# A decoder layer on one core: the feed-forward's quantised input turned by a transfer, its products moved behind other work

## The reference

```python
def activation_quant(x):                      # a row to 8 bits
    s = 127 / clip(max(abs(x), axis=-1, keepdims=True), 1e-5)
    return clip(round(x * s), -128, 127) / s

def ffn(x, w_gate, w_up, w_down, ln_weight):  # weights: ternary, scaled by mean(abs(w))
    h = silu(activation_quant(x) @ qw_gate.T) * (activation_quant(x) @ qw_up.T)   # 256 -> 1024
    h = rms_norm(h, ln_weight)
    return activation_quant(h) @ qw_down.T    # 1024 -> 256

x = x + mixer(layernorm(x), ...)              # projections x, z, B, C, dt; conv; ssd; gate; rms; W_out
x = x + cross_attention(layernorm(x), ctx_2048, ...)
x = x + ffn(layernorm(x), ...)
```

## Time and profile before

| | us |
|---|---|
| median of 3 runs | 1201.06 (1199.09 to 1201.66) |
| the profiled execution, time | 1197.11 |
| its span, first to last instruction | 1195.0 |
| PE busy | 1130.4 (95%) |
| DVE busy | 1003.0 (84%) |
| POOL busy | 930.7 (78%) |
| ACT busy | 824.2 (69%) |

### The profile page before, as it was taken

How to read it: one execution, slowest core, us unless ns; L and a number is a source line. 1 busy time by engine, 2 the same in 40 slices (tenths; PEclk the granted TensorE clock), 3 DMA queues, 4 the chain that set the end, 5 groups by cost and what they waited for, 6 DMA issues and landing times.

```text
span 1195.0 us, 34853 instructions
## 1 busy us (share of the span) xinstructions
PE 1130.4 (95%) x11463; PEld 976.4 (82%) x11463; DVE 1003.0 (84%) x2509; ACT 824.2 (69%) x2095; POOL 930.7 (78%) x1514
## 2 busy tenths in 40 slices
PE   4899999999999999999999999999999999999964
PEld 3678888889888888988888898888889888888743
DVE  4767898898889888888989888898988889888666
ACT  4686677776677776667777666677766667776642
POOL 4788778888777888877888887788888778877551
PEclk8999999999999999999999999999999999999987
DMA  8310111111110101111010111101011110111010
GB/s 292 90 50 24 33 20 31 27 35 35 31 35 22 26 26 35 35 31 35 19 29 26 35 35 31 35 16 32 26 35 35 31 35 13 35 24 27 19 10 22
DMA packets 94952, 44.39 MB, mean 37 GB/s; under 512 B 72000, under 2 KB 93248, under 8 KB 94656
## 3 DMA queue, kind: packets, MB, share of 16 engines
q1 hardware_dynamic: 91984, 43.85, 14.1%
q10 hardware_dynamic: 2928, 0.03, 0.1%
HBM read 23.93 MB, written 4.19 MB: 24 GB/s over the span
## 4 chain that ended last, share of the span: by engine, by line
PE 64%; DVE 14%; ACT 8%; issue 7%; POOL 4%; DMA 2%; DVEq 0%; SPq 0%; POOLq 0%; ACTq 0%
PE bank L1782 18%; PE bank L1672 6%; PE bank L1673 6%; PE bank L1674 6%; PE bank L1842 5%; PE bank L1700 4%; PE bank L1754 4%; PE bank L1709 4%; PE bank L1918 2%; ACT qT L868 2%; PE bank L1689 2%; DVE hh L1362 2%; DVE hh L1369 2%; PE bank L1901 2%; DVE o_lo L1294 2%
## 5 line engine op out<-in xcount | busy, mean ns | idle before, releaser
L1782 PE MATMUL bank<-xcT,wq 128*128 128x128 f32 x2048 | 234.1, 275 | 1.5 <-ACT xcT L843 1.5
L1782 PEld LDWEIGHTS bank<-xcT,wq 128*128 128x128 f32 x2048 | 231.2, 192 | 2.1 <-issue 1.8
L1205 DVE SCALAR_TENSOR_TENSOR xc<-bank,cw,xc 128x124 f32<-128x124 f32 (+2 forms) x576 | 163.8, 339 | 11.4 <-ACT xc L812 2.9
L497 POOL TENSOR_TENSOR rq<-rq,minus_half 128x16 f32<-128x16 f32 x32 | 93.9, 2935 | 88.9 <-DVE rq L1306 88.9
L1672 PE MATMUL bank<-wo_hi,o_hi 128*128 128x256 f32 x512 | 149.1, 291 | 0.0
L1673 PE MATMUL bank<-wo_lo,o_hi 128*128 128x256 f32 x512 | 143.8, 281 | 0.0
L1674 PE MATMUL bank<-wo_hi,o_lo 128*128 128x256 f32 x512 | 143.6, 280 | 0.0
L868 ACT ACTIVATE qT<-bank,bqT 128x128 f32<-128x128 f32 x384 | 109.6, 372 | 41.3 <-PE bank L1782 41.3
L511 POOL TENSOR_TENSOR pr<-pr,mask 128x512 f32<-128x512 f32 x64 | 80.0, 1272 | 30.1 <-DVE pr L1313 30.0
L1672 PEld LDWEIGHTS bank<-wo_hi,o_hi 128*128 128x128 f32 x512 | 96.6, 189 | 0.1
L1673 PEld LDWEIGHTS bank<-wo_lo,o_hi 128*128 128x128 f32 x512 | 96.6, 189 | 0.1
(11 more groups left out here) (239 smaller groups left out, 3388.2 us busy)
## 6 DMA issues: line engine op xcount, KB each, us to landing
x_in<-in_x SPq DMA_DIRECT2D x32, 128.0 KB, 2.1
c_in<-in_ctx SPq DMA_DIRECT2D x32, 128.0 KB, 2.1
x_m<-in_x SPq DMA_DIRECT2D x32, 128.0 KB, 2.2
out<-x SPq DMA_DIRECT2D x32, 128.0 KB, 1.7
wq<-in_L_xattn_Wq SPq DMA_DIRECT2D x1, 2048.0 KB, 14.1
stage<-in_L_xattn_Wo SPq DMA_DIRECT2D x2, 1024.0 KB, 8.1
w_in<-in_L_attn_W_in SPq DMA_DIRECT2D x1, 1024.0 KB, 6.3
qT<-in_L_ffn_w_gate SPq DMA_DIRECT2D x1, 1024.0 KB, 13.4
```

Of the source, the lines that this page charges most:

```text
L497: g.tensor_tensor(rq[:, 1, :], rq[:, 0, :], minus_half[:, :], ALU.pow).then_inc(s["x_rq"].sem, 1)
L1205: last = v.scalar_tensor_tensor(out=o, in0=src, scalar=cw[:, j, TAPS - 1 - back:TAPS - back], in1=o, op0=ALU.mult, op1=ALU.add)
L1782: last = mm(x_Qbank[g][:, (n % 4) * P:(n % 4 + 1) * P], wq[:, c, n * HD:(n + 1) * HD], xcT[:, c, :], start=(c == 0), stop=(c == DC - 1))
```

## The change

Tiles 1 to 29 no longer have `f_qb` transposed on PE and copied by ACT. SP's queue does it with one transposing transfer `f_qb` to `f_qT` (`turn_f`), placed between the store and `turn_m`. DVE waits, before it overwrites `f_qb`, for the transfer of the tile before. Tile 0 and the two tiles of the tail (30, 31) keep the old way.

On PE, `m_project_bc` goes directly behind `x_keys`; then come `x_sums`, `f_up` half 0, `x_sums_turn`, `x_values`, `f_up` half 1, `m_output`. On ACT both `f_tanh` go later and `m_dt_exp` earlier. On DVE `m_dt`, `x_q_mean` and `m_total` go ahead of `f_gate` half 0, half 1 goes behind `m_dt_ratio` and `x_vb_add`, and `f_weight` behind the mixer's residual and its statistics. On POOL `m_rms` goes ahead of `x_rms`.

```diff
+        F_TURN = 1
+        def by_dma(t):
+            return not isinstance(t, int) or F_TURN <= t < TILES - 2
...
+            def turn_f(t):
+                after(sp, s["f_q2"], t + 1)
+                sp.sem_inc(s["sp_waited"].sem, 1)
+                after(sp, s["f_U1"], t)
+                sp.sem_inc(s["sp_waited"].sem, 1)
+                count(sp, s["f_qturned"], (t - F_TURN) * 16)
+                sp.sem_inc(s["sp_waited"].sem, 1)
+                sp.dma_start_transpose(f_qT[:], f_qb[:]).then_inc(s["f_qturned"].sem, 16)
...
                     store(i - 4)
+                if not isinstance(i, int) or F_TURN + 3 <= i < TILES + 1:
+                    turn_f(i - 3)
                 if not isinstance(i, int) or M_TURN <= i + 2 < TILES:
                     turn_m(i + 2)
...
             def second(ms, mn, m, xa, xb, f, fb):
+                if m is not None:
+                    m_rms(m)
                 if xa is not None:
                     x_rms(xa)
-                if m is not None:
-                    m_rms(m)
...
-                if f is not None:
+                if f is not None and not by_dma(f):
                     f_T_copy(f)
...
-                if f is not None:
-                    f_tanh(f, 0)
                 if m is not None:
                     m_square(m)
...
                 if xa is not None or m is not None:
                     x_sums_copy(xa, m)
                 if f is not None:
-                    f_tanh(f, 1)
-                if xa is not None:
-                    x_k_square(xa, xb)
+                    f_tanh(f, 0)
                 if mn is not None:
                     m_dt_exp(mn)
+                if xa is not None:
+                    x_k_square(xa, xb)
                 if f is not None:
+                    f_tanh(f, 1)
                     f_square(f)
                     f_keep(f)
...
                 after(dve, s["f_q1"], t + 1)
+                if not isinstance(t, int) or t > F_TURN:
+                    count(dve, s["f_qturned"], (min(t, TILES - 2) - F_TURN) * 16 if isinstance(t, int) else (t - F_TURN) * 16)
                 v.tensor_scalar(f_qb[:], f_xn[:], ROUND, None, ALU.subtract).then_inc(s["f_q2"].sem, 1)
...
-                    after(pe, s["f_qTc"], t + 1)
+                    if by_dma(t):
+                        after(pe, s["f_x3"], t)
+                        count(pe, s["f_qturned"], (t - F_TURN + 1) * 16)
+                    else:
+                        count(pe, s["f_qTc"], pe_turn(t) + 1)
...
-                if f is not None:
+                if f is not None and not by_dma(f):
                     f_transpose(f)
                 if xa is not None:
                     x_keys(xa)
+                if mn is not None:
+                    m_project_bc(mn)
+                if xa is not None or m is not None:
+                    x_sums(xa, m)
                 if f is not None:
                     f_up(f, 0, xb)
                 if xa is not None or m is not None:
-                    x_sums(xa, m)
+                    x_sums_turn(xa, m)
+                if xa is not None:
+                    x_values(xa)
                 if f is not None:
                     f_up(f, 1, xb)
-                if xa is not None or m is not None:
-                    x_sums_turn(xa, m)
-                if mn is not None:
-                    m_project_bc(mn)
-                if xa is not None:
-                    x_values(xa)
```

More of the change, by code:

```diff
@@ L220, in decoder_layer @@
           m_tap m_convb+m_conva m_tb+m_ta m_bc+m_xs m_G m_Gm+m_Ma m_Xtr m_Xdt m_xd
-          m_Y m_y+m_yf m_sq m_ssy m_v4+m_ry m_out m_x1 m_planes m_turned c_planes c_turned c_xT
+          m_Y m_y+m_yf m_sq m_ssy m_v4+m_ry m_out m_x1 m_planes m_turned c_planes c_turned c_xT f_qturned
           x_hold x_copy x_stats+x_mean x_veps+x_rstd x_xn x_T x_TT x_K+x_V x_kb+x_vb x_ksq x_kv+x_rk+x_kh
@@ L252, in decoder_layer, with pe_turn @@
         W_CONV, W_RATE, W_SKIP, W_QK, W_SMALL, W_ATTN = 2, 2, 3, 2, 3, 2
+        F_TURN = 1
+        def by_dma(t):
+            return not isinstance(t, int) or F_TURN <= t < TILES - 2
+        def pe_turn(t):
+            return t if t < F_TURN else t - (TILES - 2 - F_TURN)
         block = ctx.enter_context(nc.Block())
@@ L905, in f_T_copy @@
             def f_T_copy(t):
-                after(act, s["f_T"], t + 1)
+                count(act, s["f_T"], pe_turn(t) + 1)
                 sc.copy(f_qT[:], turn_bank(t)[:, 0:P].bitcast(BF16).rearrange("p (c n) -> p c n", c=DC)).then_inc(s["f_qTc"].sem, 1)
@@ L1107, in body @@
                 if f is not None:
-                    f_tanh(f, 1)
+                    f_tanh(f, 0)
+                if mn is not None:
+                    m_dt_exp(mn)
                 if xa is not None:
                     x_k_square(xa, xb)
-                if mn is not None:
-                    m_dt_exp(mn)
                 if f is not None:
+                    f_tanh(f, 1)
                     f_square(f)
@@ L1597, in body @@
                     x_kv(xa)
+                if xb is not None:
+                    x_o_low(xb, 1, 0)
+                if mn is not None:
+                    m_dt(mn)
+                if xa is not None:
+                    x_q_mean(xa)
+                if m is not None:
+                    m_total(m)
                 if f is not None:
@@ L1600, in body @@
                     f_value(f, 0)
-                if xb is not None:
-                    x_o_low(xb, 1, 0)
-                if f is not None:
-                    f_gate(f, 1)
-                if xa is not None:
[L1606 to L1612, removed]
                 if mn is not None:
@@ L1617, in body @@
                 if f is not None:
-                    f_weight(f)
+                    f_gate(f, 1)
+                    f_value(f, 1)
                 if m is not None:
@@ L1622, in body @@
                 if f is not None:
+                    f_weight(f)
                     f_highest(f)
```

1 line of the change is left out of this document (removed).

## The result

The changed kernel takes 1191.34 us in the median (1190.93 to 1192.35), against 1200.8 us of the kernel before in runs beside it: a ratio of 0.9934, 95% interval 0.9921 to 0.9947, so 6.4 to 9.5 us faster. The prediction was 1189.5 us, 11.4 us faster. The profiled execution took 1191.23 us with a span of 1189.5 us (before: 1197.11 and 1195.0).

What follows compares the result with a forecast made beforehand. PE, busy 95% of the span, was taken as the bound; the DVE and ACT chain left 0.34 of 0.84 us an iteration. 8.8 us from iterations 4 to 29 plus 0.8, 1.2 and 0.6 gave 11.4 us: 1189.5 us, range 1176 to 1201.

Steps and rivals of the forecast that it cites:

- PE alone reaches `x_k_turn`: PE from `m_mix` to `x_k_turn`: +14.38 instead of +15.22 if nothing else waits.
- transposes with their wait: PE ahead of the keys: two `f_qb` squares and the wait for DVE's `f_qb` go, 0.37 us an iteration.
- the other waits (0.27 and 0.2): PE: the up product of half 1 waiting for `f_value`, 0.27 us, and smaller waits taken as 0.2 us, go.
- transfer issued, landed: SP's queue: issued 0.31 us after `f_qb`, landing 2.25 us later at +3.24, 1.3 us before the gate product wants it.
- gate product half 0, `x_sums_turn`: PE's new starts from `m_mix`: gate and up of half 0 at +4.57, `x_sums_turn` at +5.45.
- `x_k_turn`, its wait: PE's keys' transposes start at +14.88, waiting 0.5 us for the keys at the end of the DVE and ACT chain.
- gain an iteration in the loop: `m_mix` to `m_mix`: 0.34 us gained instead of 0.84, about 34.56 us instead of 34.90; 8.8 us over iterations 4 to 29.
- Behind `x_k_turn` PE's work is unchanged: PE after the keys' transposes: same work, so the 0.34 us gained at `x_k_turn` is the gain an iteration.
- My reason for iteration 30: ACT in iteration 30: no `ms`, so no x split (0.5 us less) in the chain; gain 0.8 us.
- all of PE's gain is kept: Rival at `x_k_turn`: shorter chain, no wait for keys, 28 x 0.84 = 24 us, 1177 us; chance 0.15.
- the gain is eaten: Rival in the DVE and ACT chain: a longer chain gives the old iteration, 1199 to 1203 us; chance 0.15.
- The late transfer: Rival before gate product half 0: landing beyond 3.6 us costs 9 us, 1210 us; chance 0.13, shared with a longer chain.

Runs made afterwards that it cites:

- keys early: The changed kernel with the keys' scaling (x_khat) and z's tanh moved ahead of the two splits on ACT: 1180.91 us, ratio 0.9852 to the kernel before.
- keys early, with and without transfer: The kernel with x_khat and z's tanh ahead of the splits, 1180.91 us, and the same with all tiles turned on PE, 1189.16 us.
- the add moved: The changed kernel with DVE's x_vb_add behind f_gate and f_value of half 1 instead of ahead of them: 1191.5 us, ratio 0.9938.
- one and two more transfers: The changed kernel with one or two unread copies of the f_qb transfer queued ahead of the one that counts: 1195.18 us and 1235.21 us.
- the early keys in the kernel before: The kernel before with only x_khat and z's tanh moved ahead of the two splits on ACT: 1207.98 us, ratio 1.0075.

## Where the prediction was right and wrong

The time fell inside the range, and the direction and the mechanism were right. The predicted gain (11.4 us, measured 9.5) was too large, in these steps:

| step | predicted | measured |
|---|---|---|
| PE alone reaches `x_k_turn` | +14.38 | +14.41 (keys early) |
| transposes with their wait | 0.37 | 0.30 (keys early, with and without transfer) |
| the other waits (0.27 and 0.2) | 0.47 | 0.51 |
| transfer issued, landed | +0.99, +3.24 | +0.99, +3.36 |
| gate product half 0, `x_sums_turn` | +4.57, +5.45 | +4.66, +5.54 |
| `f_value` half 1 ends | +9.97 | +9.95 |
| `x_khat` ends | +14.84 | +14.91 |
| `x_k_turn`, its wait | +14.88, 0.5 | +14.96, 0.43 |
| gain an iteration in the loop | 0.34 | 0.21 |

**The term that was mis-sized** is the gain of 0.34 us an iteration; it measured 0.21. 0.08 us of the difference is the end of the chain. `x_sums_turn` came 0.09 us late, 0.06 of it because I let the keys start at +0.56 instead of +0.62, but DVE's hand-over, its two short steps and `m_dt_ratio` took less than I had summed, and `f_value` of half 1 ended at +9.95, 0.02 early. Behind it the hand-over to ACT took 0.12 us (585.19 less 585.07) where my sum left 0.05, ACT's steps up to z's tanh 3.08 instead of 3.05, and `x_k_turn` stood at +14.96 instead of +14.88.

The other 0.055 us contradict the sentence "Behind `x_k_turn` PE's work is unchanged": from `x_k_turn` to the next `m_mix` it was 19.68 us and is 19.74 us. All of it stands at `x_k_turn` itself. Where its four matmuls waited for `kb`, their row is 0.66 us long and the next matmul starts 0.41 us behind the first of them; where they didn't wait, these are 0.60 and 0.36. The traces of the other runs divide in the same way: 19.73 to 19.74 us in the five others with the wait (the orders without the transfer, POOL's order back, the add moved, one and two more transfers), and 19.68 in the transfer without the orders, which has no wait. What a waiting group does differently is not shown.

Two smaller things: no row stood behind the 0.44 us that the sum gave DVE to see `x_sums_turn`; it measured 0.42. And `h_qb` was to be ready 0.5 us earlier; it was 0.37.

**Iteration by iteration**, from `x_k_turn` to `x_k_turn` in the two traces: iterations 4 to 29 gain 5.65 us (8.8 predicted; 0.21 each, somewhat more at the start), iteration 30 0.09 (0.8), iteration 31 0.66 (1.2), iteration 32 0.91 (0.6). My reason for iteration 30, no x split in the chain, did show: `x_k_turn` went there from +14.92 to +14.40. But iteration 29, from `m_mix` to `m_mix`, is 0.16 us longer than before (35.70 against 35.54), and `x_k_turn` to `x_k_turn` had little left. The reason is a slow transfer: `turn_h` of iteration 29 landed 4.94 us after its issue (4.38 before; 2.7 in the iterations ahead), and PE's down product waited for it. Before and after, the only such wait between 540 and 1080 us:

```profile
PE bank L1918 <- DMA h_q<-h_q: 0.5, 1, 0.5
```

```profile
PE bank L1940 <- DMA h_q<-h_q: 0.9, 1, 0.9
```

Why these landings are slow is open. The tail, counted at 0, gives 0.52 us back. Up to iteration 3, also counted at 0, the kernel after is 1.24 us later, and here something came in that I had not thought of. Granted clock of PE in the window 40 to 60 us (window, its length, busy times and instructions of PE, PEld, DVE, ACT and POOL, clock, DMA share, GB/s), before and after:

```profile
40.00:60.00 20.00, 15.85 (x173) 13.40 (x172) 15.56 (x33) 13.51 (x37) 18.87 (x26) 1.00 0.15 48
```

```profile
40.00:60.00 20.00, 16.53 (x168) 13.62 (x166) 15.63 (x32) 12.21 (x29) 18.81 (x27) 0.91 0.12 42
```

Both profiles have one stretch at 1.2 GHz in the fill ahead of this window; the profile after has a second, short one in it. No row of the fill that I read tells why: of the profiles with the new orders, the one with POOL's order back and the one with two more transfers have it too, and those with the early keys, with the values' add moved, with one more transfer and of the orders alone don't. With it, the first and the third `m_mix` lie 61.86 us apart, in the run with the values' add moved 60.55: it costs 1.3 us, about the 1.24 us of the fill. So 1.24 - 5.65 - 0.09 - 0.66 - 0.91 + 0.52 = -5.55 us is the difference of the two spans. Without the stretch I estimate 6.9 us (5.55 + 1.3), within the interval of the timed runs.

**From the profiled execution to the median.** I carried over that the profiled execution of before lay 3.95 us under its median. It lies at the low end of that kernel's runs (1196.47 to 1201.66), and the one of after is 0.11 us from its median. So the predicted 1185.7 us for a profiled execution was missed by 5.5 us, and the median by 1.8. Part of the closeness of the median is luck.

**The rivals.** That all of PE's gain is kept fell for the changed kernel: PE does arrive at +14.4, but needs ACT's list turned round to use it, and even then DVE holds the iteration at 34.33 us instead of 34.06 (34.90 less 0.84). That the gain is eaten did not come true: of the lead of 0.34 us 0.21 were left. The late transfer stayed away, with landings of 2.3 to 2.8 us; its threshold and slope were right. By the measured 0.04 us from landing to matmul it decides at 4.66 - 0.04 - 0.99 = 3.63 us (3.6 predicted), and behind that the full lateness goes into `x_k_turn`. Two squares land in 2.37 us here. The Trainium skill (VectorE: DVE Perf Modes, "The three transpose paths") gives 1309 ns for one; the 2.6 us for two in a row is an estimate from that figure, and the measured time is below it. The advice of the Trainium skill on the same page (VectorE: DVE Perf Modes, "Rules for kernel authors") to use TensorE when a PSUM destination is acceptable agrees with the runs where the transfer is uncovered (+0.85 us an iteration with the old orders), and not where 1.3 us of cover lie behind it (-0.32, and -0.30 with the keys early). That the rule compares latencies, as the prediction has it, is my reading; the page gives one time for a square and does not say which.

**Of my expectations behind the prediction** five missed in whole or in part: the early keys in the kernel before (0.3 us an iteration dearer), the values' add (neither its gain nor its loss), the size for the orders alone, the size for the early keys without the transfer (between theory and rival), and the size for two more transfers (0.16 us an iteration more). Of the changed orders only POOL's was taken back by itself; what each of the moves on PE, ACT and DVE is worth alone is not shown.

## What to carry to other kernels

When steps are moved ahead of a bottleneck engine's wait, write out the whole chain over the other engines to the next thing that this engine waits for, hand-overs included: here it kept 0.55 of 0.81 us from arriving. Then look on that chain for work that only feeds transfers and put it last; on ACT that was worth as much as the whole change. A transfer in place of a transpose paid here only together with an order that covers it, and then its gain was the engine time that it freed (0.30 us of PE), not a matter of its latency.

## What was not expected of the hardware

- Landing hardly depends on size here: 2.37 us for 128x256, 2.4 us for 128x512 and 2.7 us for 128x1024. I had drawn the trend down to 2.25. These are rows from the middle of the loop and medians. Near its start and end single transfers were slower: `turn_h` took 3.62 and 3.37 us in iterations 4 and 5, 4.94 and 4.25 in 29 and 30.
- In the middle of the loop transposing transfers queued behind one another each keep their latency: 2.34 and 2.42 us for two, 2.34, 2.38 and 2.42 us for three. In iteration 4 they don't (4.17 us, above). Only their issue, 1.24 us each, adds up.
- A group of four small transposes that had to wait for its input showed 0.66 us instead of 0.60, and the matmul behind it came 0.055 us later, in every trace that has the wait.
- The second stretch at 1.2 GHz in the fill, in some profiles of nearly the same program and not in others, cost 1.3 us, as much as six iterations of this change gain.
